# Tokens scattered by expert pair, and a feed-forward that computes two experts a tile

## The reference, cut to what matters

```python
scores = jnp.einsum('bsd,de->bse', x, gate_w) + gate_b        # x: normed tokens, 4 scores each
probs = jax.nn.softmax(scores, axis=-1)
topk_vals, topk_idx = jax.lax.top_k(probs, 2)
mask = jnp.sum(jax.nn.one_hot(topk_idx, 4), axis=-2)
masked = probs * mask
masked = masked / (jnp.sum(masked, axis=-1, keepdims=True) + 1e-09)
h = gelu(jnp.einsum('bsd,edh->ebsh', x, w1) + b1)              # 96 -> 384, for each expert
y = jnp.einsum('ebsh,ehd->ebsd', h, w2) + b2                   # 384 -> 96
out = jnp.einsum('bse,ebsd->bsd', masked, y)                   # then t + out
```

## Time and profile before

| engine | busy us | share of the span | instructions |
|---|---|---|---|
| TensorE, matmuls | 611.8 | 89% | 6885 |
| TensorE, weight loads | 450.4 | 66% | 6885 |
| VectorE | 528.6 | 77% | 1383 |
| ScalarE | 491.2 | 72% | 843 |
| GpSimd | 79.2 | 12% | 132 |

### The profile page before, as it was taken

The page is one execution under the profiler, slowest core; times in us unless marked ns, Lnnn a source line. Parts: engine busy times, 40 slices in busy tenths (PEclk is TensorE's granted clock), DMA queues, the critical chain, the costliest instruction groups (busy, mean ns, idle before and its releaser), DMA issues.

```text
span 685.0 us, 19911 instructions
## 1 busy us (share of the span) xinstructions
PE 611.8 (89%) x6885; PEld 450.4 (66%) x6885; DVE 528.6 (77%) x1383; ACT 491.2 (72%) x843; POOL 79.2 (12%) x132
## 2 busy tenths in 40 slices
PE   2467999899999999999988878999999999999995
PEld 1245687687777778777776756566666666666663
DVE  6574568678888888888877476888888888888885
ACT  1535467567777777777766346889898989899983
POOL 6000101210122211112211121300000000000000
PEclk9998569879999999999999559999999999999998
DMA  4755553454555655556550113334333333333430
GB/s 96 147 108 101 88 102 88 86 100 91 110 104 102 108 108 108 108 106 110 86 105 9 42 32 93 81 92 97 92 92 94 95 95 95 92 92 92 99 86 23
DMA packets 57596, 62.65 MB, mean 91 GB/s; under 512 B 37528, under 2 KB 48346, under 8 KB 56026
## 3 DMA queue, kind: packets, MB, share of 16 engines
q1 hardware_dynamic: 57562, 62.21, 44.3%
HBM read 40.02 MB, written 12.71 MB: 77 GB/s over the span
## 4 chain that ended last, share of the span: by engine, by line
PE 55%; DVE 21%; issue 8%; SPq 5%; DMA 5%; ACT 3%; POOLq 1%; POOL 1%; DVEq 1%; ACTq 0%
PE ps L839 6%; PE ps L816 5%; PE ps L840 5%; SPq L407 5%; PE ps L818 5%; PE ps L817 5%; PE ps L771 5%; DMA k_split<-parts_dram 4%; PE ps L831 3%; DVE neg_max L1230 2%; PE ps L688 2%; PE ps L665 2%; PE ps L810 2%; PE ps L709 2%; PE ps L781 2%
## 5 line engine op out<-in xcount | busy, mean ns | idle before, releaser
L1538 DVE TENSOR_TENSOR hidden_part<-hidden,hidden_part 128x512 fp32r<-128x512 f32 x192 | 128.5, 688 | 43.6 <-ACT hidden_part L1151 35.8
L1150 ACT ACTIVATE hidden<-ps,up_bias 128x512 f32<-128x512 f32 x192 | 132.5, 690 | 28.9 <-PE ps L840 28.9
L1151 ACT ACTIVATE hidden_part<-ps,up_bias 128x512 fp32r<-128x512 f32 x192 | 131.3, 684 | 0.0
L839 PE MATMUL ps<-in_a,up_a 128*128 128x512 f32 x192 | 83.1, 433 | 0.0
L816 PE MATMUL ps<-hidden_part,down_part 128*96 128x512 f32 x192 | 76.5, 398 | 1.8 <-DVE hidden_part L1538 1.7
L1230 DVE TENSOR_REDUCE neg_max<-ps 128x12 f32<-128x768 f32 x64 | 61.0, 953 | 21.8 <-PE ps L688 20.2
L840 PE MATMUL ps<-in_b,up_b 128*128 128x512 f32 x192 | 75.9, 395 | 0.0
L818 PE MATMUL ps<-hidden_part,down_part 128*96 128x512 f32 x192 | 75.7, 394 | 0.0
L817 PE MATMUL ps<-hidden_part,down_part 128*96 128x512 f32 x192 | 75.1, 391 | 0.0
L1032 ACT ACTIVATE probs<-ps 128x768 f32<-128x768 f32 x64 | 51.5, 805 | 30.9 <-PE ps L709 30.9
L1024 ACT ACTIVATE q_packed<-ps 24x768 bf16<-24x768 bf16 x64 | 51.4, 803 | 12.0 <-PE ps L697 9.9
(11 more groups left out here) (168 smaller groups left out, 1156.4 us busy)
## 6 DMA issues: line engine op xcount, KB each, us to landing
mix_rows<-mix_dram SPq DMA_DIRECT2D x16, 768.0 KB, 5.3
parts_dram<-parts_room SPq DMA_DIRECT2D x32, 288.0 KB, 2.6
q_packed<-parts_dram SPq DMA_DIRECT2D x96, 96.0 KB
k_split<-parts_dram SPq DMA_DIRECT2D x192, 48.0 KB
in_c<-in_a SPq DMA_DIRECT2D x64, 64.0 KB, 4.3
x_in<-in_x SPq DMA_DIRECT2D x64, 48.0 KB, 4.5
x_res<-in_x SPq DMA_DIRECT2D x64, 48.0 KB, 4.3
out<-out_sb SPq DMA_DIRECT2D x64, 48.0 KB, 2.0
```

The costliest lines, as they stand in the source:

```text
L839: pe.matmul(up_bank(u, n), up_a[:, e, cols], in_a[u][:, :], start=False, stop=False)
L1150: act.activation(hidden[n % 4][:, :], up_bank(u, n), ACT.Gelu, bias=bias).then_inc(hidden_ready, 1)
L1151: act.activation(hidden_parts[n % 4][0][:, :], up_bank(u, n), ACT.Gelu, bias=bias)\
L1538: dve.tensor_tensor(hidden_parts[n % 4][1][:, :], hidden[n % 4][:, :], hidden_parts[n % 4][0][:, :].bitcast(F32), ALU.subtract).then_inc(h ...
```

## The change: what it does, and the diff

The feed-forward computes, for each token, only its two experts. Tokens are sorted by expert pair on the way through DRAM:

- In attention each block's tokens get a place. A new stage `tail_c`, one iteration behind `tail_b`, ranks the four scores on GpSimd (`choose`, 24 instructions), marks the token's pair, and computes the shares. Three small matmuls (`ranks`) count the tokens of each pair that came before; VectorE picks the position (`positions`). GpSimd then writes 128 rows at a time to the DRAM buffer `xs`, each row to its own position, by an indirect transfer (`scatter_rows`, four a block). A row is 800 bytes: normed token, residual row, four shares, place in the output. `xs` has a region of 9216 rows for each pair.
- When 13 blocks are placed, VectorE builds the table of the first 8 tiles (`assign_early`); with all 16 it builds the rest, always 21 tiles in all (`assign_late`). A table entry holds a tile's first row, its two experts, and for each whether it differs from that of the tile two before. Unfilled ends of the regions are overwritten with rows that lead nowhere (`pad_groups`, six stores and a wait for them, after the sixth tile's step in SyncE's queue).
- The split weights are stored to DRAM once (`w_dram`, 12 stores of 3 MB in all). A tile's two experts are loaded into one of two sets of buffers (`load_w`), three transfers an expert, 754 KB, and each is skipped where the expert is the one already there.
- A tile's input is no longer in SBUF. SyncE loads the normed tokens (`load_h`), TensorE transposes them (`turn_in`), and packing has six moves. The other half of the rows is loaded by `load_r` into `tile_r`, which also holds the places that the scatter of the results reads.
- A tile has six units. For each expert TensorE transposes the result back (`turn_out`), VectorE weighs and adds it (`weigh`: two instructions an expert), and GpSimd scatters the tile to the output's rows (`scatter_out`, four indirect transfers of 128 rows).
- GpSimd's copy of `h2T` and the shares' way through DRAM go. ScalarE and VectorE read the two experts' numbers into registers at each tile (`experts`), for the bias.

```diff
-NFT = NB * N // FT
-LAG = 3
-QUADS = NE * CH // 4
-IN_MOVES = 7
+LANES = 3
+REGION = TOKENS + 1024
+ROW = 2 * C + 8
+TILES = TOKENS // FT + NG - 1
+EARLY_BLOCKS = NB - 3
+EARLY = EARLY_BLOCKS * N // FT - (NG - 1)
+IN_MOVES = 3 + LANES
...
 SyncE, ahead of the loop over blocks
+            for e in range(NE):
+                for rows_of, cols in ((128, slice(0, UP_C)), (LANES * REST, slice(UP_C, DOWN)), (128, slice(DOWN, WROW))):
+                    sp.dma_start(w_dram[e, 0:rows_of, cols], w_parts[0:rows_of, e, cols].bitcast(F32))\
+                        .then_inc(w_stored, 16)
...
 SyncE, feed-forward
+            def load_w(t, k, u, i):
+                if not (isinstance(t, int) and t < 2):
+                    sp.wait_ge(down_done, CH * (2 * t + i - 3))
+                e, changed = entry(t, 1 + i, NE - 1), entry(t, 3 + i, 1)
+                for rows_of, cols in ((128, slice(0, UP_C)), (LANES * REST, slice(UP_C, DOWN)), (128, slice(DOWN, WROW))):
+                    sp.dma_start(w_expert[u][i][0:rows_of, cols].bitcast(F32),
+                                 w_dram[bass.ds(e, 1), 0:rows_of, cols].rearrange("e p n -> (e p) n"), cond=changed)\
+                        .then_inc(w_loaded[u][i], 16)
+            def load_h(t, u):
+                if not (isinstance(t, int) and t < 2):
+                    sp.wait_ge(in_turned, t - 1)
+                src = xs[bass.ds(row_of(t), FT), 0:C].rearrange("(q a) c -> q a c", a=FP)
+                load(tile_h[u][:, :, :], src, tile_h_loaded[u])
+            def load_r(t, k, u):
+                if not (isinstance(t, int) and t < 2):
+                    sp.wait_ge(out_stored[u], 16 * FP * k)
+                src = xs[bass.ds(row_of(t), FT), C:ROW].rearrange("(q a) c -> q a c", a=FP)
+                load(tile_r[u][:, :, :], src, tile_r_loaded[u])
...
+            def step(t, k, u):
+                if not (isinstance(t, int) and t + 2 >= TILES):
+                    load_h(t + 2, u)
+                load_r(t, k, u)
+                if not (isinstance(t, int) and t + 1 >= TILES):
+                    for i in range(2):
+                        load_w(t + 1, k + u, 1 - u, i)
+                if not (isinstance(t, int) and t + 2 >= TILES):
+                    pack_input(t + 2, u)
...
+            for t in range(EARLY - 2):
+                step(t, t // 2, t % 2)
+            pad_groups()
+            tiles(sp, EARLY - 2, TILES - 3, step)
...
 GpSimd
+            def scatter_rows(k, u):
+                pool.wait_ge(position_ready, nth(k, u))
+                pool.wait_ge(h2_ready, nth(k, u))
+                pool.wait_ge(shares_ready, 2 * nth(k, u))
+                if not is_first(k):
+                    wait_apart(rows_stored[u], 16 * NP * k)
+                for p in range(NP):
+                    pool.indirect_dma_start(
+                        out=xs[:, :], out_offset=bass.IndirectOffsetOnAxis(ap=position[u][:, p:p + 1], axis=0),
+                        in_=rows[u][:, p, :], in_offset=None).then_inc(rows_stored[u], 16)
+            def scatter_out(t, k, u):
+                wait_apart(half_ready, 2 * t + 2)
+                for a in range(FP):
...
             def iteration(k, u, norm, project, attend, tail_a, tail_b, tail_c):
+                if tail_c:
+                    choose(*after(k, u, -3), loaded_exps)
                 if norm:
                     gn_rstd_of(*after(k, u, 2))
...
+                if tail_c:
+                    scatter_rows(*after(k, u, -3))
...
+            choose(NB // 2 - 1, 0, loaded_exps)
+            iteration(NB // 2, 1, False, False, False, False, True, False)
+            scatter_rows(NB // 2 - 1, 0)
+            scatter_out(0, 0, 0)
+            choose(NB // 2 - 1, 1, power_exps)
+            scatter_out(1, 0, 1)
+            scatter_rows(NB // 2 - 1, 1)
+            tiles(pool, 2, TILES - 1, scatter_out)
...
 TensorE, feed-forward
+            def tile(t, k, u, late=None):
+                for i in range(2):
+                    turn_out(t - 2 + i, 1 - i)
+                    down(t - 1, 1 - u, i, 1)
+                    down(t - 1, 1 - u, i, 2)
+                    main(t, k, u, i, 0)
+                    main(t, k, u, i, 1)
+                    if i == 0:
+                        down(t - 1, 1 - u, 1, 0)
+                    else:
+                        down(t, u, 0, 0)
+                    main(t, k, u, i, 2)
...
+                    if i == 1 and not (isinstance(t, int) and t + 2 >= TILES):
+                        turn_in(t + 2, u, None if late is None else NB)
+                    up_rests(t, u, i)
...
 VectorE, feed-forward
+            def weigh(t, k, u, i):
+                g = 2 * t + i
+                share = tile_r[u][:, :, bass.ds(SHARES - C + expert(u, i), 1)].broadcast_to([128, FP, C])
+                dve.wait_ge(out_turned, g + 1)
+                if i == 0:
+                    dve.wait_ge(tile_r_loaded[u], 16 * (k + 1))
...
+                dve.tensor_tensor(y_weighed[:, :, :], out_ps, share, ALU.mult).then_inc(y_weighed_ready, 1)
+                dve.wait_ge(y_weighed_ready, g + 1)
+                dve.tensor_tensor(out_sb[u][:, :, :], y_weighed[:, :, :],
+                                  out_sb[u][:, :, :] if i else tile_r[u][:, :, 0:C], ALU.add).then_inc(half_ready, 1)
...
+            def tile(t, k, u):
+                load_experts(t, u)
+                for i in range(2):
+                    if i == 1 and not (isinstance(t, int) and t + 2 >= TILES):
+                        input_rest(t + 2, k + 1, u)
+                    weigh(t - 1, k - 1 + u, 1 - u, i)
+                    unit(t, k, u, i)
```

More of the change, by code:

```diff
@@ L845, in when, with iteration @@
+            def iteration(k, u, norm, project, attend, tail_a, tail_b, tail_c):
+                n, j, a, b, c = [after(k, u, by) for by in (2, 1, -1, -2, -3)]
                 def when(there, step, *args):
@@ L986, in _ @@
+            tiles(pe, EARLY - 2, TILES - 3, tile)
+            for t in range(TILES - 3, TILES):
+                tile(t, t // 2, t % 2)
+            last = TILES - 1
+            turn_out(last - 1, 1)
+            down(last, last % 2, 0, 1)
+            down(last, last % 2, 0, 2)
+            down(last, last % 2, 1, 0)
+            turn_out(last, 0)
+            down(last, last % 2, 1, 1)
+            down(last, last % 2, 1, 2)
+            turn_out(last, 1)
         @blk.scalar
@@ L1171, in _ @@
-            tile(NFT - 1, 1)
+            for t in range(EARLY - 2):
+                tile(t, t // 2, t % 2)
+            act.wait_ge(table_ready, 2)
+            tiles(act, EARLY - 2, TILES - 3, tile)
+            for t in range(TILES - 3, TILES):
+                tile(t, t // 2, t % 2)
         @blk.vector
@@ L1378, in copy_mix @@
-            def copy_mix(half):
-                dve.wait_ge(mixT_ready, half + 1)
-                dve.tensor_copy(mixT[:, half, :], mixT_ps[half]).then_inc(mixT_copied, 1)
-            def iteration(k, u, norm, project, attend, tail_a, tail_b):
-                n, j, a, b = after(k, u, 2), after(k, u, 1), after(k, u, -1), after(k, u, -2)
-                drained = tail_a and not attend
+                n = nth(k, u)
+                dve.wait_ge(gate_ready, n)
+                dve.tensor_reduce(g_top[:, :], gate_ps, AX.X, ALU.max).then_inc(g_top_ready, 1)
@@ new lines, in unit, with tile @@
+            def unit(t, k, u, i):
+                hidden_rest(t, u, i, 0)
+                if i:
+                    take_y(t, u, 0)
+                elif not is_first(t):
+                    take_y(t - 1, 1 - u, 1)
+                hidden_rest(t, u, i, 1)
+                hidden_rest(t, u, i, 2)
+            def tile(t, k, u):
+                load_experts(t, u)
+                for i in range(2):
+                    if i == 1 and not (isinstance(t, int) and t + 2 >= TILES):
+                        input_rest(t + 2, k + 1, u)
+                    weigh(t - 1, k - 1 + u, 1 - u, i)
+                    unit(t, k, u, i)
@@ new lines, in first_tiles @@
+                weigh(2, 1, 0, 0)
+                unit(3, 1, 1, 0)
+                positions(*last_block, 1)
+                assign_late()
+                input_rest(5, 2, 1)
+                weigh(2, 1, 0, 1)
+                unit(3, 1, 1, 1)
+            first_tiles()
+            for t in range(4, EARLY - 2):
+                tile(t, t // 2, t % 2)
+            tiles(dve, EARLY - 2, TILES - 3, tile)
+            for t in range(TILES - 3, TILES):
+                tile(t, t // 2, t % 2)
+            last = TILES - 1
```

934 lines of the change are left out of this document (573 added, 361 removed).

## The result

The changed kernel takes 753.88 us (median of 4 runs, 751.47 to 759.09); the kernel before took 677.45 in the runs beside it. The ratio is 1.112, with a 95% interval from 1.104 to 1.119: 11% slower. I had forecast 703, also slower, but by 26 us where it is 76. The profiled execution spans 751.5.

The account below looks back on a forecast made before the run. TensorE's pace bounded both long stages before; afterwards SyncE's queue, behind scatters, would bound the tile. Before's 404.3, 9.0 and 9.9, a 252 stage, and additions of 3, 8, 10, 12 and 3 gave 711, or 703 us median; range 652 to 770.

Parts of the forecast that it names:

- to the first up matmul: Span before the feed-forward: 404.3 before, +3 at the start, +8 in attention, +10 between the stages.
- 21 steady tiles: Feed-forward stage: between 248 and 260 us, taken as 252, against 261.8 before.
- interleaving and stops: Early feed-forward: 9.0 of interleaving with the last block stays; two new stops, padding stores and choose, +6 each.
- end: After the tiles: 9.9 as before, plus 3 because results leave through weighing, scatter and landing.
- SyncE's work: Feed-forward tile: fourteen issues at 0.65 and six value reads at 0.45 take 11.8 us.
- the chain: Feed-forward: the next tile's loads stand behind a scatter; period at least 10.85, or 13.85 where the first expert changes.
- What the change takes out: Feed-forward tile: six units instead of twelve; 9.3 us for TensorE, floor 9.6, compute period 10.3.
- Attention: Thirteen iterations: VectorE's new operations add 0.6 a block, 8 in all; GpSimd's choose, 8.3, hidden at D = 1.0.
- carry-over of -8: Whole kernel: the median of the runs lies 8 below the profiled span, so 711 becomes 703.
- Rival 1: Feed-forward: neither scatter chain nor SyncE binds, TensorE nearly sets the tile; 661 on the median; chance 0.32.
- Rival 2: GpSimd slow, 1.36 or more per scatter; stage 276, GpSimd's round reaches attention's block; 730 on the median; chance 0.21.
- Rival 3: Feed-forward: the clock may fall to half, a tile taking 17 or more; about 800; chance 0.05.

Follow-up runs that it names:

- e2: Against the changed kernel: an expert's split weights move in one transfer instead of three, stored and loaded; 748.8 us, ratio 1.098.
- e1: Against the changed kernel: SyncE issues the residual load at the end of its step, behind weights and packing; 753.8 us, ratio 1.109.
- e3: Against the changed kernel: weight loads, their register reads and waits left out from the third tile on; 710.0 us, ratio 1.043.
- e4: Against the changed kernel: GpSimd scatters the results of tile 0 ahead of the rows of block 14; 759.2 us, ratio 1.116.
- e9: Against the changed kernel: SyncE issues the next tile's weights ahead of the residual load, and that load ahead of the packing; 740.4 us, ratio 1.090.
- e12: Against the changed kernel: two more unused register reads at the end of each of SyncE's steps; 769.0 us, ratio 1.129.
- e13: e10 plus ScalarE's weight stores, GpSimd's padding and reordered work, and the first two tiles turned and packed inside attention's last iteration; 688.2 us, ratio 1.006.
- e10: e9 with one transfer an expert, register reads without the bounds test, and the row read once; 711.6 us, ratio 1.045.
- e5: Against the changed kernel: the edits of e1 and e2 together; 743.6 us, ratio 1.086.
- e6: e5 with register reads without the bounds test and a tile's row read once; 737.6 us, ratio 1.078.

## Why the prediction was right in direction and wrong in size

By its own steps, in the span (forecast 711, measured 751.5; the end is what the last first up matmul has behind it beyond a steady tile, the stops are what the twenty tiles before it take beyond steady ones):

| step | forecast | measured |
|---|---|---|
| to the first up matmul: 404.3 + 3 + 8 + 10 | 425 | 420.9 |
| 21 steady tiles | 252 | 286 |
| interleaving and stops, 9.0 + 12 | 21 | 28.8 |
| end, 9.9 + 3 | 12.9 | 15.6 |

- **The step that failed is the stage of 252**, 34 of the 40 us: the tile is 13.63 and not 12.0. Both mechanisms were named, both sizes were short.
  - I had 11.8 for SyncE's work and measured 12.9: a read 0.69 instead of 0.45 (+1.4), address arithmetic at the loads and the loop (+0.9, not priced), a skipped transfer about 0.35 instead of 0.65 (-1.0), and executed issues slightly under 0.65.
  - In the chain I had 10.85, and 13.85 where the first expert changes, 11.7 on average; where e2 leaves it to bind, with two issues less in it, the tile is 12.94 (11.9 and 14.6). In the link shown above four scatters take 5.0 instead of 4.0 (a scatter is 0.97, as taken, but the next begins 1.28 after it), the landing 2.2 instead of 2.0 (SyncE's wait ends at 611.7), SyncE's part 3.4 (I had 3.95, of which the two issues less leave 2.65), and the weights land 3.9 after their issue instead of 3.
  - And I chose 252 between 248 and 260 as if a late tile were partly made up later. The measured stage lies above that whole range; how much of a late tile is made up, no run tells apart.
- That SyncE is hardly idle, that its waits are led by the residual load, that TensorE waits for weights at a tile's first matmul, that a tile is longer where the first expert changes: all seen (the steady tiles lie between 10.7 and 16.9; the five with such a change take 15.2 on average, the others 12.7).
- What the change takes out was right: 10.2 to 10.6 a tile once SyncE is out of the way, against 10.3.
- Attention was near: the choice takes 8.4 on GpSimd (8.3 forecast) and hides; blocks take 0.36 more (0.6 forecast). The stores at the start delay the first packing by 13.5 and its keys by 10 (87.15 to 97.20, forecast 4), but the next blocks give a part back: block 16 begins 6.8 late, where I had 11. From there to the first up matmul another 9.8 over before (10 forecast). That the sum fits so well is in part luck: e1, e3, e4, e9 and e12 leave all of this as it is, and in their profiles block 16 begins 9.7 to 16.4 late, and the first up matmul comes at 423.0 to 434.9. Only the 20.65 of a steady block is the same in all of them. e13 shows that the turn's part could be had back.
- There were two stops, as I had it, each with 11 over a steady tile instead of 6; with the interleaving they make 28.8. The padding's is as named. The one at the fourth tile was not the choice that I had named, but the rows of block 14, which waited for VectorE's positions; the choice came up behind them when e4 changed the order.
- The carry-over of -8 from the span to the median was wrong: after the change the runs' median lies 2.4 above the profile's span. That is 10 of the 51 between 703 and 754. In every execution on record that lists both, the time is 1.6 to 1.9 above the span; so the profiled 685.0 was an execution of some 687 (an estimate), longer than all four beside the result (675.8 to 681.5). I had taken that one's surplus for a constant.
- Rival 1 needed cheap issues; e10 shows its tile (10.62, turning point 10.8), and that even with it the fixed costs leave no gain (711.6, where rival 1 had 661). Rival 2's price (730) came nearer than the forecast, by its larger spacing of scatters; GpSimd's round in attention stayed hidden, against it. Rival 3 is there in part: the granted clock was 0.91 in the steady tiles, 1.00 in those of e3 and 0.99 in those of e10. It rose when the waits went, so it followed them; what it adds to a tile of its own, no run tells apart.
- The Trainium skill's "DMA: Bandwidth & Descriptors" (Anatomy of one DMA, SWDGE path) puts most of a GpSimd DMA's 2.0 us behind its issue. The trace agrees in the share, not in the sum: a scatter of 100 KB takes a median of 3.3 us from issue to landing, and the next one begins on GpSimd after 1.28. The same page (Latency and other measured facts) gives about 600 ns as the floor of a `tensor_load`; this trace shows 0.27 for the load of a table entry from SBUF alone and about 0.69 with what surrounds it, and the trace decides.

## What to carry to other kernels

The engine that only issues transfers is an engine with a budget: count its issues, its register reads and their arithmetic per step, and compare the sum with the step that is hoped for. Where two limits lie within one us of each other, taking away one shows nothing; take away both before either is acquitted. And when an experiment moves a load out of the way, look first whether its consumer now waits: e1, e5 and e6 misled me until I read VectorE's waits.

## What the runs showed of the hardware that I had not expected

- A transfer that is skipped by its condition costs SyncE 0.07 to 0.09 us itself, but about 0.35 with the arithmetic that is done all the same.
- GpSimd's closing instruction, the drain, is long. In the kernel before it took 5.9 us at 430.5, under the feed-forward; after the change GpSimd is the last engine to finish, and the drain stands at the end. The rows of the line that ends the program, first of the kernel before, then of the one after:

```profile
L72 POOLq DRAIN  x1: 5927/5927/5927, 430.5 to 430.5; - x1
```

```profile
L66 POOLq DRAIN  x1: 10672/10672/10672, 740.6 to 740.6; - x1
L66 SPq DRAIN  x1: 13/13/13, 745.3 to 745.3; - x1
```

After the change it begins at 740.6 and ends at 751.3, six us after SyncE's own last steps, which wait for the results to land (745.3). In all profiles with the change it ends 5 to 6 us after that. The end is 15.6 instead of 9.9; no run takes this drain away, so that these six us are the excess is read from the rows, not tested.
